# A GRU over 50 steps and its product with the vocabulary: the order of the steps, one lane of 512 rows at a time in two halves

## The reference

```python
x = emb_table[input_ids]                      # 2048 x 50 x 128
xp = x @ kernel + b_i                         # 2048 x 50 x 384
for t in range(50):
    rec = h @ rec_kernel + b_r
    z = sigmoid(xz + rz); r = sigmoid(xr + rr)
    hh = tanh(xh + r * rh)
    h = z * h + (1 - z) * hh
logits = h_last @ emb_table.T                 # 2048 x 12501, 102 MB
```

## Time and profile before

| | us |
|---|---|
| median of three runs | 1208.89 (1208.09 to 1209.45) |
| the profiled execution | 1205.95 |
| its span, first to last instruction | 1204.1 |
| PE busy | 1064.9 (88%) |
| DVE busy | 798.4 (66%) |
| POOL busy | 763.7 (63%) |
| ACT busy | 693.7 (58%) |

### The profile page before, as it was taken

How to read it: one execution, slowest core, us unless ns; L and a number is a source line. 1 busy time by engine, 2 the same in 40 slices (tenths; PEclk the granted TensorE clock), 3 DMA queues, 4 the chain that set the end, 5 groups by cost and what they waited for, 6 DMA issues and landing times.

```text
span 1204.1 us, 17546 instructions
## 1 busy us (share of the span) xinstructions
PE 1064.9 (88%) x6031; PEld 804.9 (67%) x6031; DVE 798.4 (66%) x1481; ACT 693.7 (58%) x1203; POOL 763.7 (63%) x812
## 2 busy tenths in 40 slices
PE   7968777877777778777899999999999999999997
PEld 6964444444444444444588888888888888888775
DVE  5745555555555555555677777888888887777644
ACT  4443444444444444444477777777777788888543
POOL 0017777777777777777777777777777777663000
PEclk9989999999999999999999999999999999999999
DMA  8986565656565656565588889989899999997799
GB/s 259 350 320 175 167 175 166 176 166 175 167 176 167 175 167 175 166 175 167 169 258 288 290 295 297 297 294 297 291 296 291 296 298 331 310 306 270 257 356 324
DMA packets 127495, 294.29 MB, mean 244 GB/s; under 512 B 18096, under 2 KB 33456, under 8 KB 127408
## 3 DMA queue, kind: packets, MB, share of 16 engines
q0 software_dynamic: 51200, 157.34, 45.3%
q1 hardware_dynamic: 76208, 135.84, 31.2%
HBM read 171.30 MB, written 121.81 MB: 243 GB/s over the span
## 4 chain that ended last, share of the span: by engine, by line
PE 56%; POOL 26%; issue 11%; DMA 5%; DVE 1%; ACT 0%; SPq 0%; DVEq 0%; ACTq 0%
POOL gathered L369 26%; PE x_ps L452 6%; PE x_ps L453 6%; PE x_ps L454 6%; PE r_ps L419 3%; DMA out_dram<-logits 3%; PE c_ps L419 3%; PE r_ps L432 3%; PE z_ps L432 3%; PE z_ps L419 3%; PE r_ps L433 2%; PE r_ps L436 2%; PE c_ps L432 2%; PE c_ps L433 2%; PE c_ps L436 2%
## 5 line engine op out<-in xcount | busy, mean ns | idle before, releaser
L369 POOL DMA_INDIRECT gathered<-gate_table,index x800 | 761.8, 952 | 338.1 <-issue 229.4
L570 ACT ACTIVATE table_rows<-r_ps,zr_bias 128x512 f32<-128x512 f32 (+1 forms) x250 | 151.2, 605 | 200.7 <-PE r_ps L427 162.6
L704 DVE SCALAR_TENSOR_TENSOR c_ps<-c_ps,bias_sb,table_rows 128x512 f32<-128x512 f32 (+1 forms) x250 | 162.8, 651 | 132.1 <-PE c_ps L427 98.6
L572 ACT ACTIVATE z_ps<-z_ps,zr_bias 128x512 f32<-128x512 f32 (+1 forms) x250 | 144.2, 577 | 182.4 <-PE z_ps L427 143.0
L562 ACT ACTIVATE logits<-x_ps,nan_row 128x512 f32<-128x512 f32 (+1 forms) x325 | 214.4, 678 | 42.8 <-PE x_ps L454 27.9
L709 DVE TENSOR_TENSOR table_rows<-z_ps,state 128x512 f32<-128x512 f32 (+1 forms) x250 | 145.0, 580 | 113.6 <-ACT z_ps L572 113.4
L419 PE MATMUL r_ps<-ident,gathered 128*128 128x128 f32 x800 | 107.6, 248 | 119.3 <-issue 107.6
L713 DVE SCALAR_TENSOR_TENSOR c_ps<-z_ps,table_rows 128x512 f32<-128x512 f32 (+1 forms) x250 | 147.7, 591 | 59.8 <-ACT table_rows L579 59.4
L419 PEld LDWEIGHTS r_ps<-ident,gathered 128*128 128x128 f32 x800 | 84.9, 141 | 138.2 <-issue 131.5
L716 DVE TENSOR_TENSOR state<-table_rows,c_ps 128x512 f32<-128x512 f32 (+1 forms) x250 | 145.3, 581 | 26.1
L579 ACT ACTIVATE table_rows<-c_ps,bias_sb 128x512 f32<-128x512 f32 (+1 forms) x250 | 149.7, 599 | 16.2 <-PE c_ps L419 14.7
(11 more groups left out here) (97 smaller groups left out, 1538.8 us busy)
## 6 DMA issues: line engine op xcount, KB each, us to landing
out_dram<-logits SPq DMA_DIRECT2D x192, 512.0 KB, 4.5
gate_table<-table_rows SPq DMA_DIRECT2D x24, 768.0 KB, 5.5
gathered<-gate_table,index POOLq DMA_INDIRECT x800
emb_rows<-in_L_rec_emb_table_dram SPq DMA_DIRECT2D x48, 256.0 KB, 5.8
out_dram<-logits SPq DMA_DIRECT2D x8, 213.0 KB, 3.7
logits<-in_r_input_ids_dram SPq DMA_DIRECT2D x1, 400.0 KB, 4.8
logits<-in_r_input_mask_dram SPq DMA_DIRECT2D x1, 400.0 KB, 6.2
gate_table<-table_rows SPq DMA_DIRECT2D x2, 192.0 KB, 9.3
```

What stands on the lines that cost most here:

```text
L369: nc.gpsimd.indirect_dma_start(tile_rows(slot, n).bitcast(F32), None, table, bass.IndirectOffsetOnAxis(ap=index[:, tile, b.t:b.t + 1], axi ...
L570: nc.scalar.activation(r, r_bank, ACT.Sigmoid, bias=zr_bias[:, 1:2]).then_inc(s_r, 1)
L704: nc.vector.scalar_tensor_tensor(out=c_bank, in0=c_bank, scalar=bias_sb[:, 1, 2:3], in1=r, op0=ALU.add, op1=ALU.mult).then_inc(s_scaled, 1)
```

## The change

`schedule` writes another order. Each lane runs by itself, lane 0 first, as its two halves in turn: 100 blocks of 256 rows for each lane, 400 in all. From block 100 on (lane 1) the products are split (`split_from` is 2 * T as before, but now it is the first block of lane 1). Every even block from 100 on carries a pair, 150 as before, and the pairs come lane by lane, so those of lane 0 run beside lane 1, and those of lane 3 are the 50 of the tail. The vocabulary stands beside every fourth block as before, and these are now blocks of 256.

```diff
-    lanes = [(lane, 0, LANE) for lane in range(LANES)]
-    a, b = (3, 0, HALF), (3, HALF, HALF)
-    order = [lanes[0], lanes[1]] * T + [lanes[2], a, lanes[2], b] * (T // 2) + [a, b] * (T - T // 2)
-    return order, 2 * T, lambda g: g >= 2 * T, [range(0, 4), range(4, 6), range(6, 8)]
+    order = []
+    for lane in range(LANES):
+        order += [(lane, 0, HALF), (lane, HALF, HALF)] * T
+
+    def carries(g):
+        return g >= 2 * T and g % 2 == 0
+
+    return order, 2 * T, carries, [range(2 * lane, 2 * lane + 2) for lane in range(LANES)]
```

## The result

The changed kernel takes 1290.84 us (median of four runs, 1289.93 to 1292.54), the one before 1209.17 beside it. The ratio is 1.0675, with a 95% interval of 1.0659 to 1.0691. The forecast was 1287, in a range of 1257 to 1316. The profiled execution took 1290.82, its span is 1288.7.

What follows compares the result with a forecast made beforehand. A chain of waits of 5.79 us per step was taken to bound lanes 1 to 3. Lane 0 to 340.7, these lanes to 1201.1, the tail to 1282.0, then 1.85 and 2.94 gave 1287 us, range 1257 to 1316.

Steps and rivals of the forecast that it cites:

- The bound of A: Kernel before: stage A, 4.98 us per block, goes at POOL's pace of four gathers, 5.00; B and C at PE's.
- The loop: Lanes 1 to 3: chain of waits through a plain and a loaded block, 5.79 us per time step, the longest bound.
- Lanes 1 to 3: Line 704 of block 100 to that of 399: 149 steps of 5.79 plus 3.42, 866.1 us, less 5.7.
- The first steps of a lane: Two pairs of the narrow chunk at each start of lanes 1 to 3 save 0.95 us each, 5.7 in all.
- Lane 0: First 100 blocks, no split or pairs: stays at POOL's pace, 5.0 us per step; line 704 of block 100 at 340.7.
- Rival 3: Lane 0 falls off POOL's pace: chunk work over 10 us per four blocks, 12 to 31 us more; 8%.
- The engines' work: Lanes 1 to 3, per step: PE 4.59 us, DVE 4.48, ACT 3.7, all under POOL's 5.00.
- The tail: The last 50 pairs, behind the last line 704: 81.17 us as before, less 0.3.
- The sum: Whole kernel: span 1282.0 us, 1283.9 with 1.85 around it, then 2.94 more for the median, 1287; +6.5%.
- The clock: PE's granted clock stays 1.00 (2.4 GHz) in lanes 1 to 3; rival that it halves: well over 1400 us, 2%.
- POOL setting the pace: Rival: the loop closes in 5.00 us or less, lanes 1 to 3 go at 5.0 per step, median about 1174; 5%.
- The plain block that costs as much as a loaded one: Rival in lanes 1 to 3: a plain block takes 2.99 us as in stage C, median 1318; 7%.

Runs made afterwards that it cites:

- experiment 6: The kernel before with half of the gathers left out, zeros standing for the second 128 of every 256 rows: 1091.76 us.
- experiment 8: The changed kernel with the third matmul left out of every unit beside a block: 1238.58 us (1479.02 on the chip with the falling clock).
- experiment 4: The changed kernel with one unit of a pair beside each block and its copy behind the tanh on ACT: 1180.21 us.
- experiment 1: The changed kernel without the 150 pairs beside the blocks, the tail's 50 kept: 1179.13 us.

## Why the prediction was right, point by point

**The bound of A** (POOL) and of B and C (PE): shown by experiment 6.

**The loop.** Forecast 5.79 per step, measured 5.80; the parts 2.37 and 3.42, measured 2.36 and 3.44. Every link came out within 0.03 of the earlier trace rows: line 708 to c's transposes 0.54, pair to copies 0.89 (704.76 - 703.87), copies to tanh 1.29, tanh to line 717 0.49, on to line 708 0.88. The sum rested on the first blocks of C, which show these links before PE fills up: all blocks of C carry a pair, but that of the first one is narrow, so PE had to wait for its line 704 (0.27) as it does behind a plain block. One term was read wrongly without harm to the sum: on the loop are both units on PE and one copy, not one unit and two copies (experiment 8).

**Lanes 1 to 3.** 860.4 forecast from line 704 of block 100 to that of block 399, 862.96 measured (line 708, 341.79 to 1204.75). 149 steps times 0.01 are 1.5. The first steps of a lane saved a little less than the 0.95 each that I took (2.60 + 2.35 and 2.50 + 2.35 in lane 3, so 0.85 and 0.95, and 2.75 + 2.36 in lane 1's first, so 0.69). Five steps were 0.12 to 0.15 longer.

**Lane 0.** Line 704 of block 100 was forecast at 340.7, and line 708 came at 341.79. The number was near, but the reason given doesn't hold: the lane is not at POOL's pace. Line 708 comes three times at 2.33 and once, beside a chunk, at 2.87, so four blocks take 9.87 against POOL's 10.0, and behind its first block PE waited for rows three times in the whole lane, 2.0 us. Block 100's last gather began at 335.69, and line 708 followed 6.10 later, where rows just in time would have made it 4.4. I had 10.1 per four blocks as POOL's pace and a little. Both bounds lie so near each other that the time can't tell them apart, and that it came out within 1.1 us is luck. The mean over the lane is 2.51 per block, because the first blocks and a few others are late. Rival 3 (later than 350) is excluded.

**The engines' work.** PE's 727.28 in 149.5 steps is 4.86 per step as recorded, 4.59 forecast. It also pauses differently than I said, not in several pieces but once per step: 0.93 us before c's transposes of the plain block (702.16), and then it works on to 707.05. It is no bound either way.

**The tail.** 80.9 forecast, 83.95 measured. Part of it is at its start: after its pauses at the last blocks (0.93, 0.38 and 1.16 us) PE ran its first units at half speed for some 3 us (matmuls of 512 columns recorded as 0.63 instead of 0.39, about 1.6 us in all). Where the other 1.4 went is open; the copies' waits for the output transfers add up to 52.8 us instead of 48.6.

**The sum.** The three stretches came out 1.1, 2.5 and 3.1 us longer than forecast, 6.7 in all (a span of 1288.7 against 1282.0), and the execution 6.9 (1290.82 against 1283.9). The median came closer, 1290.84 against 1287, since I had added 2.94 for a profiled run faster than the median, which this one was not. That part is luck.

**The clock.** 1.00 in lanes 1 to 3, as assumed from A. It is not a matter of course, see the last section.

**The rivals.** POOL setting the pace (1174) was priced rightly as what a loop under 5.00 would give: experiment 4 is that case, at 1180. What it takes was named in the prediction too, work on ACT or PE that slips out of the loop. The plain block that costs as much as a loaded one is excluded by 2.36 and by experiment 1.

## What to carry to other kernels

When all engines go through the same list of steps in order, look for the loop through the order (here DVE, PE, ACT, DVE), and sum it from start to start over a step with extra work and one without; the busy shares (84% at most here) don't show it. Extra work that fills one step and leaves the next empty costs more than the same work spread: the same pairs, one unit in each block and its copy behind the tanh, brought 1290.8 to 1180.2. The first steps of a stage, before the busiest engine fills up (here three blocks at the start of C), show the links of a loop that the rest of the stage hides, and so give the price of an arrangement that the trace doesn't otherwise hold.

## What the runs showed of the hardware

The granted clock of TensorE differed from chip to chip for the same program. On one chip the kernel with two matmuls per unit (one run on each) had, from 300 us on, PE busy 759 of 1000 us and a clock of 0.90; on another it had 652 of 800 us and 1.00. The rows, first chip and then second (columns as in the earlier trace rows):

```profile
300.00:1300.00 1000.00, 759.31 (x5023) 664.37 (x5021) 676.83 (x1769) 569.26 (x1193) 577.31 (x611) 0.90 0.63 191
```

```profile
300.00:1100.00 800.00, 652.24 (x4943) 583.17 (x4942) 650.27 (x1745) 557.97 (x1170) 570.37 (x601) 1.00 0.78 239
```

On the first chip, the timeline of PE and ACT at the start of one such stretch:

```profile
602.21 0.28 PE L440 MATMUL r_ps<-state_lo,w_rec_hi 128*128 128x256 f32 x1
...
605.22 0.47 ACT L578 ACTIVATE table_rows<-r_ps,zr_bias 128x256 f32<-128x256 f32 x1 [2.47 <-remote]
...
606.36 0.49 PE L423 MATMUL c_ps<-ident,gathered 128*128 128x128 f32 x2 [3.20 <-DVE c_ps L712]
...
609.72 0.63 PE L458 MATMUL x_ps<-embT_lo,state_hi 128*128 128x512 f32 x1
```

r's product is recorded as done at 602.49, but its sigmoid starts at 605.22, with no releaser that the profile knows; PE was idle 3.20 us before 606.36, and its next matmuls went at the lower level, 1.2 GHz (0.63 for 512 columns). Since the ends of matmuls are modelled in the record, it doesn't tell whether the pause came first or a lower clock that it doesn't show.

That kernel took 1479.02 us there and 1238.58 on the other chip, while the one that keeps PE full (experiment 6) had a clock of 1.00 from 96 to 1009 us on the same chip, and its stage C took 146.99 us against 146.63 elsewhere. The rule that the prediction set against its rows (the Trainium skill, "TensorE: Matmul & The Clock Gate", section "A second HAM failure mode: psum-queue depth-cycling": frequent short pauses make the clock swing) may be at work on the first chip, but isn't shown there, since the stretch above begins with one long pause; in lanes 1 to 3 of the changed kernel, with a pause of 0.93 us in each step and a clock of 1.00, it didn't show. The clock also fell where the times were as usual, but behind single longer pauses: 1.60 us in experiment 1 (two blocks at 3.12 follow, and a granted clock of 0.96 over the lanes) and 1.16 us at the start of the changed kernel's tail. Why the same kernel ran so differently on two chips stays open.
